# Eight tiles of logits computed at the head of attention, and attention and dispatch in one block

## The reference

```python
xn = layernorm(x)
att = softmax(causal(q @ k.T / 4));  a = (att @ v) @ wo.T
y = layernorm(xn);  logits = y @ se.T                # 2048 x 1024 for each sequence
dispatch = softmax(logits, over rows);  combine = softmax(logits, over slots)
slots = dispatch.T @ y;  eout = (gelu(slots @ Wg + bg) * (slots @ Wu + bu)) @ Wd + bd
out = x + a + combine @ eout
```

## Time and profile before

| | us |
|---|---|
| median of 3 runs (lowest, highest) | 2695.19 (2692.81, 2697.54) |
| profiled execution, its own time | 2698.62 |
| its span, first to last instruction | 2696.9 |
| head of attention: first to last of steps -22 to -1 on TensorE | about 158.9 to 202.2 |
| steps of attention | about 202 to 1758 |
| L(0) and L(1) on ScalarE, first to last copy | 1767.4 to 1869.7 |

### The profile page before, as it was taken

The page is one execution under the profiler, slowest core; times in us unless marked ns, Lnnn a source line. Parts: engine busy times, 40 slices in busy tenths (PEclk is TensorE's granted clock), DMA queues, the critical chain, the costliest instruction groups (busy, mean ns, idle before and its releaser), DMA issues. The chain is left out here.

```text
span 2696.9 us, 47797 instructions
## 1 busy us (share of the span) xinstructions
PE 2583.9 (96%) x16291; PEld 1542.2 (57%) x16291; DVE 2048.5 (76%) x4879; ACT 1728.3 (64%) x3510; POOL 427.1 (16%) x676
## 2 busy tenths in 40 slices
PE   7989999999999999999999999998989989999999
PEld 4544444444444444444444444376877878889999
DVE  7779889989998998998898998477465513356665
ACT  4567777777777777777777777966666652222221
POOL 6701111111111111111111111323120100100000
PEclk9969999999999999999999999999999999999999
DMA  7945423303312321330330000044333354545654
GB/s 247 324 111 60 58 29 45 44 12 41 45 24 27 45 34 17 45 44 6 45 44 6 10 6 31 7 181 168 124 134 145 102 168 147 175 152 194 194 193 151
DMA packets 175855, 245.10 MB, mean 91 GB/s; under 512 B 57205, under 2 KB 129017, under 8 KB 174105
## 3 DMA queue, kind: packets, MB, share of 16 engines
q1 hardware_dynamic: 160088, 227.73, 33.8%
q10 hardware_dynamic: 15552, 14.68, 1.8%
HBM read 156.21 MB, written 84.97 MB: 89 GB/s over the span
## 5 line engine op out<-in xcount | busy, mean ns | idle before, releaser
L809 ACT ACTIVATE att_pr<-att_ring 128x512 f32<-128x512 f32 (+3 forms) x2560 | 1174.3, 550 | 333.9 <-PE att_ring L890 326.6
L857 DVE TENSOR_REDUCE att_mx<-att_ring 128x1 f32<-128x512 f32 x1536 | 967.5, 679 | 76.6 <-PE att_ring L903 74.2
L903 PE MATMUL att_ring<-att_ks,att_qs 48*128 48x512 f32 (+3 forms) x1920 | 648.4, 422 | 16.3 <-ACT att_pr L809 7.0
L890 PE MATMUL att_ring<-att_qs,att_ks 64*128 64x512 f32 (+3 forms) x1920 | 578.2, 407 | 5.8 <-DVE att_mx L863 2.3
L890 PEld LDWEIGHTS att_ring<-att_qs,att_ks 64*128 64x128 f32 x1920 | 300.5, 186 | 402.7 <-DVE att_mx L857 148.3
L863 DVE CUSTOM_DVE_ANT_0 att_junk<-att_ring,w_causal 128x256 bf16<-128x256 f32 (+3 forms) x1024 | 466.1, 486 | 59.5 <-PE att_ring L903 34.1
L932 PE MATMUL att_acc<-att_pr,att_v 128*17 128x512 f32 (+3 forms) x3840 | 454.3, 544 | 3.9 <-ACT att_cT L820 1.5
L903 PEld LDWEIGHTS att_ring<-att_ks,att_qs 48*128 48x128 f32 x1920 | 306.9, 185 | 141.6 <-ACT att_pr L809 102.0
L760 POOL TENSOR_SCALAR_AFFINE_SELECT att_pr<-att_pr 128x512 f32<-128x512 f32 x256 | 162.5, 635 | 1035.5 <-ACT att_pr L809 1035.4
L903 PE MATMUL att_ring<-g_ks,g_qs 48*128 48x512 f32 (+3 forms) x640 | 227.1, 465 | 15.6 <-PEq L152 5.7
L1513 ACT CAST com_e1h<-com_tp 128x1024 fp32r<-128x1024 f32 x64 | 64.8, 1017 | 236.2 <-PE com_tp L1573 236.2
(11 more groups left out here) (170 smaller groups left out, 3272.5 us busy)
## 6 DMA issues: line engine op xcount, KB each, us to landing
slot_exps<-dis_e SPq DMA_DIRECT2D x64, 512.0 KB, 2.7
com_e<-slot_exps SPq DMA_DIRECT2D x64, 512.0 KB, 3.5
att_qs<-q_parts SPq DMA_DIRECT2D x72, 256.0 KB, 12.0
q_parts<-proj_part SPq DMA_DIRECT2D x32, 512.0 KB, 5.1
dis_y<-in_L_attn_x_dram SPq DMA_DIRECT2D x64, 256.0 KB, 2.8
att_ks<-k_parts SPq DMA_DIRECT2D x72, 128.0 KB, 12.6
y_cols<-proj_yT SPq DMA_DIRECT2D x16, 512.0 KB, 5.5
context<-att_cn SPq DMA_DIRECT2D x64, 128.0 KB, 2.0
```

Source lines behind the costliest of these rows:

```text
L809: nc.scalar.activation(pr[:, s % NPR, h, off:CH], spot(("s", s, h)), ACT.Exp, scale=float(HD) ** -0.5).then_inc(exp_done, 1)
L857: nc.vector.tensor_reduce(dst, spot(e), AX.X, ALU.max).then_inc(mb_used, 1)
L890: nc.tensor.matmul(spot(e), ks[g][r, kb * P:(kb + 1) * P], qs[g][r, c, hf * CH + off:(hf + 1) * CH], start=True, stop=True).then_inc(sT_re ...
L903: nc.tensor.matmul(spot(e), qs[g][r, c, q0:q0 + P], ks[g][r, j * CH:j * CH + wd], start=True, stop=True).then_inc(mb_ready, 1)
```

## The change

- **Logits at the head.** The logits of tiles 0 to 7 of sequence 0 are computed in attention's ring, as 16 half tiles (`l` events) of 6 products each, one at the end of each of steps -18 to -3. ScalarE copies each to the buffers of probabilities, SyncE stores it to DRAM (`first_logits`), and ScalarE waits for all 16 stores before its first exponential (step 0). SyncE loads two chunks of y for it at the start, and GpSimd splits them.
- **Zeros.** GpSimd writes the zeros of groups 1 to 3 in place of ScalarE: two memsets ahead of the split, the other ten one for each step below 0, ahead of that step's part in the maxima.
- **The end of attention.** In the last 22 steps and after, VectorE makes the row maxima and the column maxima of the eight tiles, from a copy that SyncE loads back into the queries of groups 0 and 1. The chunks of y that are loaded and split ahead are now 2, 3 and 4.
- **One block.** `attend` and `dispatch` share a block; TensorE waits only for the readers of each bank. L(0) has tiles 8 to 15. SyncE loads the eight tiles again, into the logits' place (the first raises one semaphore, the other seven another). Their exponentials are spread over the 24 tiles left (`exps_by`): two after the first copy, then 1 or 2 after each.
- Queries of all groups lie in one tensor; `project` puts its parts there too.

The diff, without the lines whose indentation alone changes, cut to its core:

```diff
@@ attend
+    NL = 2 * NE                                  # NE = 8, NEC = 2
+    L_FROM = -LEAD + 4
...
+        early = [("l", s - L_FROM)] if 0 <= s - L_FROM < NL else []
...
-        out = [st[0], xs[0], st[1], xs[1]] + ev + [xs[2], st[2], st[3], xs[3]] + av
+        out = [st[0], xs[0], st[1], xs[1]] + ev + [xs[2], st[2], st[3], xs[3]] + early + av
...
+        def half_tile(k):
+            return pr[:, k // GS % NPR, k % GS, :]
...
@@ attend, sync
+            for n in range(NEC):
+                sp.dma_start(cols["low"][:, n].bitcast(F32), scr["yT_in"][0, n]).then_inc(cols["in"][n], 16)
...
+                    elif e[0] == "l":
+                        k = e[1]
+                        sp.wait_ge(l_kept, k + 1)
+                        sp.dma_start(scr["first_logits"][k // 2, :, k % 2 * 512:(k % 2 + 1) * 512],
+                                     half_tile(k)).then_inc(l_out, 16)
...
+                if s == STEPS - NU + AV_LAG:
+                    sp.wait_ge(l_out, 16 * NL)
+                    sp.wait_ge(pv_done, (NBG - 4 + -(-NE // 4)) * NU)
+                    for t in range(NE):
+                        sp.dma_start(lg[:, t, :], scr["first_logits"][t]).then_inc(l_in, 16)
@@ attend, gpsimd
+            side = zeros()                          # one memset for each next()
+            for _ in range(2):
+                next(side)
+            for n in range(NEC):
+                pool.wait_ge(cols["in"][n], 16)
+                hi, lo = cols["high"][:, n], cols["low"][:, n]
+                nc.gpsimd.tensor_copy(hi, lo.bitcast(F32)).then_inc(l_split, 1)
+                pool.wait_ge(l_split, 2 * n + 1)
+                nc.gpsimd.tensor_tensor(lo, lo.bitcast(F32), hi.bitcast(F32), ALU.subtract).then_inc(l_split, 1)
+                pool.wait_ge(l_split, 2 * n + 2)
...
+                if s < 0:
+                    made = sum(len(m_events(u)) for u in range(-LEAD, s))
+                    if made:
+                        pool.wait_ge(nm_ready, made)
+                    next(side, None)
@@ attend, scalar
-                for g in range(1, NKV):
-                    for rg in range(NRG):
-                        r = slice(RG * rg + 32, RG * (rg + 1))
-                        zero = w["causal"][r, 0:1]
-                        nc.scalar.copy(qs[g][r].rearrange("p c n -> p (c n)"),
-                                       zero.to_broadcast([32, CPB * HL * CH])).then_inc(zeroed[g], 1)
-                        nc.scalar.copy(ks[g][r], zero.to_broadcast([32, S])).then_inc(zeroed[g], 1)
...
+                for e in program(s):
+                    if e[0] == "l":
+                        act.wait_ge(mb_ready, turn[e] + 1)
...
+                        nc.scalar.copy(half_tile(e[1]), spot(e)).then_inc(l_kept, 1)
+                if s == 0:
+                    act.wait_ge(l_out, 16 * NL)
@@ attend, vector: logit_maxes(), one or two of its 16 instructions a step once no x is left
+                    next(side, None)
+                    if s % 2:
+                        next(side, None)
@@ attend, tensor
+                    elif e[0] == "l":
+                        t, h = divmod(e[1], 2)
+                        wait_bank(pe, e)
+                        pe.wait_ge(l_split, 2 * (t // TPC) + 2)
...
+                        for k in range(DK):
+                            hi, lo = cols["high"][:, t // TPC, k, at], cols["low"][:, t // TPC, k, at]
+                            nc.tensor.matmul(spot(e), hi, seTh[:, k, to], start=(k == 0), stop=False)
+                            nc.tensor.matmul(spot(e), hi, seTl[:, k, to], start=False, stop=False)
+                            last = nc.tensor.matmul(spot(e), lo, seTh[:, k, to], start=False, stop=(k == DK - 1))
+                        last.then_inc(mb_ready, 1)
@@ dispatch
+        first_tile = lambda b: 0 if b else NE
+        SLOTS = 2 * TPB - NE
+        exps_by = lambda b, t: min(-(-2 * TPB * (b * TPB + t + 1 - NE) // SLOTS), b * TPB + t)
...
+            for t in range(NE):
+                sp.dma_start(lgs[0][:, t, :], scr["first_logits"][t]).then_inc(l_in[min(t, 1)], 16)
...
-                        for t in range(TPB):
+                    for t in range(first_tile(b), TPB):
...
-                            if t > 0:
-                                token_exp(b, t - 1)
+                        token_exps(exps_by(b, t) if b < 2 else b * TPB + t)
...
+                if b == 0 and t < 2:
+                    act.wait_ge(l_in[t], 16 if t == 0 else 16 * (NE - 1))
...
+                            if b < 2 and t < (first_tile(b) if b == 0 else 0) + 2:
+                                bank_free(pe, 4 * i + 2 * (t % 2) + h)
@@ block_kernel
-            attend(nc, w, scr, g0, cols)
+            block = both.enter_context(nc.Block())
+            before = attend(nc, block, w, scr, g0, cols, queries, first_logits)
...
-            dispatch(nc, w, io, scr, pre, cols)
+            with both:
+                dispatch(nc, block, w, io, scr, pre, cols, first_logits, before)
```

More of the change, by code:

```diff
@@ L47 @@
 HL = GS // NRG
+NE = 8
+NEC = NE // TPC
+QW = CPB * HL * CH
 VW = 32
@@ L537, in load_ones, with attend @@
             yield sp.dma_start(ks[row:row + 1, :].bitcast(F32), w["ones"][0:S // 64, :].bitcast(F32)).then_inc(ones_set, 16)
-def attend(nc, w, scr, g0, cols):
+def attend(nc, block, w, scr, g0, cols, queries, first_logits):
     def chunk_units(c):
@@ L642, in place @@
             spot[1] += need
-        return where, before, {e: m[-1] for e, m in mates.items()}
+        return where, before, {e: m[-1] for e, m in mates.items()}, held
     NEAR = 4
     fills = [e for s in ALL_STEPS for e in program(s) if e[0] != "a"]
-    where, before, last_mate = place(fills)
+    where, before, last_mate, held_last = place(fills)
     turn = {e: n for n, e in enumerate(e for e in fills if e[0] != "s")}
@@ L653, in attend @@
         passed = a.sem("passed")
-        qs = [g0["qs"]] + [a.sb(f"qs{g}", [P, CPB, HL * CH], F32R) for g in range(1, NKV)]
+        qs = [queries[:, g * QW:(g + 1) * QW].rearrange("p (c n) -> p c n", c=CPB) for g in range(NKV)]
         ks = [g0["ks"]] + [a.sb(f"ks{g}", [P, S], F32R) for g in range(1, NKV)]
@@ L670, in attend @@
         loaded = [g0["loaded"]] + [sem(f"loaded{g}") for g in range(1, NKV)]
-        zeroed = [sem(f"zeroed{g}") for g in range(NKV)]
+        zeroed = sem("zeroed")
         m_rows = [sem(f"m_rows{c}") for c in range(CPB)]
@@ L682, in wait_bank, with wait_read @@
         def wait_bank(pe, e):
-            exps = [GS * x[1] + x[2] + 1 for x in before.get(e, ()) if x[0] == "s"]
-            rest = [dve_turn[x] + 1 for x in before.get(e, ()) if x[0] in "xm"]
-            kept = [x[1] * CPB + x[2] + 1 for x in before.get(e, ()) if x[0] == "c"]
+            wait_read(pe, before.get(e, ()))
+        def wait_read(pe, held):
+            exps = [GS * x[1] + x[2] + 1 for x in held if x[0] == "s"]
+            rest = [dve_turn[x] + 1 for x in held if x[0] in "xm"]
+            kept = [x[1] * CPB + x[2] + 1 for x in held if x[0] == "c"]
+            early = [x[1] + 1 for x in held if x[0] == "l"]
+            if early:
+                pe.wait_ge(l_kept, max(early))
             if exps:
@@ L942, in dispatch, with bank_free, stored @@
+        def bank_free(pe, bank):
+            if bank < NBANK:
+                wait_read(pe, held_last[bank])
+            else:
+                pe.wait_ge(cT_ready, NBG * CPB)
+        def stored(sp):
+            for c in range(CPB):
+                sp.wait_ge(c_out[c], 16 * NBG)
+        return bank_free, stored
+def dispatch(nc, block, w, io, scr, pre, cols, first_logits, before):
     HB = SB // 2
@@ L949, in dispatch @@
     half_of = lambda ph: 2 * ph[1] + ph[2]
+    bank_free, context_stored = before
     early = lambda b: range(AHEAD) if b + 1 < B else range(0)
@@ L957, in dispatch @@
         e1 = a.sb("e1", [P, 2, NS])
-        nr, zr = a.sb("nr", [P, 2, TPB]), a.sb("zr", [P, 2, TPB])
-        cm = a.sb("cm", [P, 2, NS])
+        nr, cm, nr_ready, cm_done = (first_logits[n] for n in ("nr", "cm", "nr_ready", "cm_done"))
+        zr = a.sb("zr", [P, 2, TPB])
         rz = a.sb("rz", [P, SB])
@@ new lines, in _, with split, column_maxes @@
+        @block.gpsimd
+        def _(pool):
+            def split(n):
+                if n < B * CPB:
+                    q = n % RING
+                    wait_apart(pool, yT_in[q], 16 * ((n - NEC) // RING), passed)
+                    nc.gpsimd.tensor_copy(yTh[:, q], yTl[:, q].bitcast(F32)).then_inc(yT_high, 1)
+                    pool.wait_ge(yT_high, n - RING - NEC + 1)
+                    nc.gpsimd.tensor_tensor(yTl[:, q], yTl[:, q].bitcast(F32), yTh[:, q].bitcast(F32),
+                                            ALU.subtract).then_inc(yT_split, 1)
+            def column_maxes(b):
+                wait_apart(pool, cm_done, TPB * (b + 1), passed)
+                for hf in range(2):
+                    h = slice(hf * 512, (hf + 1) * 512)
```

(12 more changed lines are left out.)

993 lines of the change are left out of this document (510 added, 483 removed).

## The result

| | before | changed |
|---|---|---|
| median (lowest, highest), runs | 2696.4 us (2692.8, 2698.1), 4 | 2724.9 us (2722.9, 2727.0), 4 |
| profiled execution, its span | 2698.6, 2696.9 | 2725.7, 2723.9 |

The change makes the kernel slower: ratio 1.0104, 95% interval 1.0091 to 1.0116, that is 28.5 us (24.5 to 31.3). The forecast had the sign and half the size (13.5), and its range ended at 2721.

The account below looks back on a forecast made before the run. VectorE was taken to bound the head, TensorE attention's steps and dispatch's first logits. Head +29 and dispatch -15.5 gave +13.5 us on 2698.6, so 2712.1; with the median 3.4 lower, 2709 us, range 2694 to 2721.

Parts of the forecast that it names:

- Head, part 1: Start of attention: GpSimd's six memsets and two splits make VectorE's copy of the first turned maxima 13 us late.
- Part 2: Head's products: eight steps at 2.2 us plus 2.2 for the clock put step -8's copy of turned maxima 16 us late.
- Rival C: Head: TensorE's clock stays at half throughout, as before; +28 us, 2723 us; chance 0.11.
- Part 3: Head's stores: the last four logits stores wait behind group 1's loads until 235.5 us; ScalarE's first exponential is 32.5 late.
- rival A: Head: stores of logits don't wait for the loads; net -3 us, 2692 us (2686 to 2697); chance 0.2.
- Part 4: First exponential to step 4's copy of turned maxima takes 9.8 us, not 13; that copy and all attention 29 us late.
- End of attention: Attention's end: added VectorE instructions fall where it has nothing to do; 0 us, up to 3 for masks made later.
- Dispatch: First logits of dispatch: tile 23 ready 18.4 us earlier, less 1.2 and 1.7; gain 15.5 us, bounds 10 to 26.
- Border: Between attention and dispatch: TensorE starts some 3.9 us earlier after the last context copy, without ten slow products.
- the ring of `e1`: Dispatch: two buffers allow an exponential every 1.97 us, 20 of them 39.4 us, ending 1.7 us later than TensorE.
- The later part of L(1): Late in dispatch's first logits: a ring of waits between ScalarE and VectorE before and after; no change counted.
- Rival E: Dispatch: loads back, y and `e1` stores press the same queue; gain only 8 to 10 us, 2716 us; chance 0.14.

Follow-up runs that it names:

- e2: Changed kernel, but GpSimd writes no zeros until the first chunk's maxima are split, then one memset a step; 2713.6 us, 1.0077 of the kernel before.
- e1: Changed kernel, but group 1 of the first sequence is loaded at step -1 instead of -6, behind all stores of logits; 2706.9 us, 1.0046 of before.
- e10: Changed kernel, but ScalarE waits for twelve stores of logits at step 0 and the last four at step 3, by two semaphores; 2717.8 us, 1.0085 of before.
- e4: Changed kernel without the second loading of the eight tiles, which are read where attention's end had put them; 2710.8 us, 1.0067 of the kernel before.
- e9: e6, but SyncE loads each chunk of y in dispatch behind the stores of `e1` of the tile after; 2678.5 us, 0.9945 of the kernel before.
- e13: Changed kernel, but SyncE loads each chunk of y behind the stores of `e1` of the tile after; 2716.8 us, 1.0079 of the kernel before.
- e6: Changed kernel with group 1 loaded at step -1, no second loading, zeros kept behind the first chunk's maxima and away from the second's; 2681.3 us, 0.9948 of before.
- e7: e6, but ScalarE instead of SyncE issues dispatch's chunks of y, in its own queue; 2680.1 us, 0.9944 of the kernel before.

## Why the prediction was wrong

Measured from each execution's own start.

- **Head, part 1**: forecast 13 late, measured 25.03 - 13.17 = 11.9. A memset took 3.50 and 1.80 us, but a split 1.04 + 2.35, less than the 1.15 + 2.82 of the earlier trace rows. e2 shows the cause. Right.
- **Part 2**: step -8 forecast 16 late, measured 46.2 - 29.9 = 16.3. In part this is luck: the turned maxima were 1.1 us less late than forecast, and the eight steps behind them took 4.4 us more than before, not 3.1. Behind the pause the clock came back, as forecast, but 5.4 us behind the first product after the pause (185.0 to 190.4), not 4.4; the stretches of the changed kernel:

```profile
180.00:185.00 5.00, 0.00 (x0) 0.01 (x1) 0.00 (x0) 0.00 (x0) 4.74 (x5) 0.52 0.00 0
...
190.00:195.00 5.00, 5.00 (x23) 3.17 (x23) 4.14 (x14) 1.17 (x2) 4.88 (x3) 0.96 0.27 105
...
225.00:230.00 5.00, 0.00 (x0) 0.00 (x0) 0.42 (x1) 0.00 (x0) 0.00 (x0) 0.50 1.05 116
```

  Rival C is out.
- **Part 3**: the loads start 50.2 us after the start (forecast 50.4), the first exponential comes 27.3 us later (forecast 26.2). e1 and e10 show the cause. Right; rival A, to which I gave 0.2, is out.
- **Part 4**: head +31.0, forecast +29. The first exponential is 33.5 us late (forecast 32.5), and from there to the mark of step 4 it takes 10.5 us (forecast 9.8, before 13.1): the clock was at half for 6.4 us behind TensorE's first product (238.6 to 245.0), where 4.4 was forecast. In e1, with 2.5 us of waiting left, the way from step -8 to step 4 takes 27.7 us, before 27.2.
- **End of attention**: +1.2, inside 0 to 3; but tails of kernels with early logits run from 38.6 to 41.3, so it tells little. By the rule of "SBUF — State Buffer" in the Trainium skill (section "Who interferes with whom") column maxima would be longer beside GpSimd: six of seven took 1.20 us and one, next to a split, 1.60. But two more splits ran beside the six, and there it was GpSimd that took longer, its subtraction 2.42 and 2.27 us against 1.28. The masks, for which the prediction had allowed 1.2 us each (three are 3.6, not its 3), took 0.64, 0.73 and 0.63. So the two do contend, and the wait fell mostly on GpSimd.
- **Dispatch, the step that failed.** Forecast -15.5, measured -10.8 to tile 23 and -7.8 to tile 31. Border, wait for the reload (tile 11 starts 17.5 us after the last context copy, forecast 16.5; no row shows the 1.5 us of latency in that sum, and the tiles were back 13.5 us after the first was issued, forecast 12.5) and its price (e4: 10.7) were right. The term mis-sized is the ring of `e1`: 1.97 us for each exponential forecast, 2.59 measured (1811.57 to 1863.45 us for 20). From the start of tile 11 to the copy of tile 23 it took 45.1 us, forecast 41.4: that is 3.7 of the 4.7 us missed there, the later start of tile 11 the rest.

  The count was wrong too: I put 20 exponentials from 1776.5 ahead of that copy, but behind the one of tile 1 (1772.6) there stand 18, up to tile 19. At 1.97 they would have ended at 1809, before TensorE's 1813.3, and cost nothing; the 1.7 us that the forecast gave the ring came from the wrong count and hid part of the miss. Nor could 1.97 be reached: TensorE makes 24 tiles of 2.80 us for 32 exponentials, one in 2.10.

  Why 2.59: I had taken the 2.7 us of the earlier trace rows, a median over a stage in which two stores stand far apart, as the landing of each. But every four tiles SyncE first waits for TensorE and then puts 512 KB of y ahead of a ready store: the store at 1819.42 us landed 5.0 us later, and the first one, issued behind the reload, 9.8. e9 and e13 show that the order makes 0.2 us of the difference. The rest I lay to the bytes of y in the queue, since with e9's order and no reload it is still 2.38 and the stores behind a chunk of y still land late; no run takes these bytes away, so its size is not shown.
- **The later part of L(1)**, to which I gave nothing, as a ring of waits the same before and after, is 3.0 us longer. ScalarE's timeline shows it catching up between tiles 23 and 24:

```profile
1863.45 1.15 ACT L1215 ACTIVATE dis_e<-dis_lg,w_nr 128x1024 f32<-128x1024 f32 x1 [2.46 <-DMA slot_exps<-dis_e]
1864.60 4.02 ACT L1195 ACTIVATE dis_y<-dis_y,w_yb,w_ys 128x256 f32<-128x256 f32 x8
1868.53 0.99 ACT L1242 COPY dis_lg<-dis_ps 128x1024 f32<-128x1024 f32 x1
```

  9.7 us between two copies where it was 6.0; in e9 and e13, where the exponentials keep up better, tiles 24 to 31 take 38 us, of 36.9 before.

Of the 15 us between forecast and result, dispatch is 7.7, the head 2.0, the tail 1.2: 10.9. The other 4 are open. In the one pair of traces 2.7 of them lie in start, loop and rest, which the change hardly touches, and the medians are 1.5 us further apart than that pair; the interval of the ratio reaches down to +24.5, which would leave nothing open. Rival E, the transfers in one queue, was the right mechanism for y and the stores, not for the tiles loaded back (e4), and its gain of 8 to 10 nearly the measured 7.8, which lies below my own bound of 10. The range reached its 2716 but not the same together with a head 2 us longer, a tail of 1.2 and the open 4: I had added E to the middle of the other terms, not to their upper ends.

## What to carry to other kernels

A transfer that something waits for must not stand behind a group of small loads nor behind the issuing engine's wait for another engine: both were free to mend by order alone (14 us for the loads in e1, about 4 for the wait in e13). Work moved into a stage with idle time on one engine has to be checked for what it puts ahead of that stage's first product on every other engine, the memsets too. And a pair of buffers is priced by the worst landing in its new company, not by the median of the old.

## What was not expected of the hardware

- A 256 KB store landed in 2.0 us on an empty queue and in 15.8 to 16.1 behind 17 loads that SyncE had begun to issue 10 us earlier.
- The first store of `e1` behind the reload took SyncE 2.44 us to issue, others 0.33.
- The y chunks landed after 4.2 us from SyncE's queue (e6) and 4.0 from ScalarE's (e7). A queue of their own cut ScalarE's waits for stores to 11.7 us, a better place in the shared one (e9) to 8.6, with the same way to tile 23.
- Stages with nearly the same instructions differed between profiled executions by 7.5 us (from launch to attention), 9 (loop) and 5.6 us (behind tile 31). In the loop most of it goes with how long the clock was at half in a busy TensorE: 6.8 to 27.3 us of 1500.
